# A convolution in 8 planes of 64 partitions: 64x64 products over 6 shifts instead of 128x128 products over 4

## The reference, cut to what matters

```python
qkv = conv2d(x, w_qkv)                       # 1x1, 256 -> 768 channels
agg = conv2d(qkv, w_dw, groups=768, pad=2)   # 5x5, each channel by itself
agg = conv2d(agg, w_pw, groups=96)           # 1x1 within groups of 8 channels
ms = concatenate([qkv, agg], axis=1)         # 64 heads of q, k, v with 8 channels each
q, k, v = split(...);  q = relu(q);  k = relu(k);  v = pad(v, one more column of ones)
kv = einsum('bgnd,bgne->bgde', k, v)
out = einsum('bgnd,bgde->bgne', q, kv)
out = out[..., :-1] / (out[..., -1:] + 1e-15)
return conv2d(out, w_proj)                   # 1x1, 512 -> 256
```

## Time and profile before

| | us |
|---|---|
| median of 3 runs | 9156.37 (9153.67 to 9159.21) |
| the profiled execution's own time | 9132.41 |
| its span, first to last instruction | 9130.6 |
| PE busy in the span | 7661.6 (84%) |
| DVE, POOL, ACT busy | 5047.8, 3797.0, 3522.8 |
| mean granted clock of PE | 0.910 |

### The profile page before, as it was taken

One profiled execution on the slowest core, in us unless ns is written; L12 is line 12 of the kernel. 1 busy time (PEld: TensorE's weight loads), 2 busy tenths in 40 slices (PEclk: granted clock), 3 DMA queues, 4 the chain that ended last, 5 costly groups with the idle time before them and its releaser, 6 DMA issues.

```text
span 9130.6 us, 206107 instructions
## 1 busy us (share of the span) xinstructions
PE 7661.6 (84%) x65004; PEld 5202.2 (57%) x65004; DVE 5047.8 (55%) x11563; ACT 3522.8 (39%) x9207; POOL 3797.0 (42%) x10084
## 2 busy tenths in 40 slices
PE   8978899788997879978899787997889978899778
PEld 5645566555565555555556555565555655555555
DVE  3475644756446564475644756447564465644656
ACT  1145621455214462144521455214452145521455
POOL 2335533355333553344533355334453344533444
PEclk9988899888998899988899889998899988999889
DMA  3201122011220112201122011220112201122111
GB/s 100 65 15 26 38 88 65 15 26 38 89 65 15 26 40 87 65 16 27 39 87 65 15 26 42 84 65 17 26 47 78 65 17 26 50 75 65 21 22 54
DMA packets 398743, 431.90 MB, mean 47 GB/s; under 512 B 159184, under 2 KB 355984, under 8 KB 393296
## 3 DMA queue, kind: packets, MB, share of 16 engines
q1 hardware_dynamic: 397648, 418.42, 16.2%
HBM read 102.76 MB, written 67.63 MB: 19 GB/s over the span
## 4 chain that ended last, share of the span: by engine, by line
PE 54%; DVE 23%; issue 7%; DMA 6%; ACT 5%; DVEq 3%; SPq 1%; POOL 1%; POOLq 0%; ACTq 0%
PE PS L621 12%; PE PS L684 7%; DVE arena L1132 5%; PE PS L902 5%; DVE arena L1222 4%; PE PS L771 4%; PE PS L867 3%; PE PS L664 3%; PE PS L827 3%; PE PS L836 3%; DVE SM L1346 3%; ACT arena L1076 2%; DVEq L1334 2%; PE PS L652 2%; DMA kv_rows<-arena 2%
## 5 line engine op out<-in xcount | busy, mean ns | idle before, releaser
L971 ACT ACTIVATE arena<-PS 128x128 f32<-128x128 f32 (+5 forms) x4160 | 1552.4, 399 | 2072.8 <-PE PS L621 598.2
L559 POOL COPY arena<-arena 64x129 f32 x6144 | 1537.7, 294 | 1386.7 <-PE PS L873 1136.1
L483 POOL TENSOR_TENSOR arena<-arena 128x512 f32<-128x512 f32 x768 | 806.4, 1072 | 1459.4 <-PE PS L621 1443.9
L621 PE MATMUL PS<-arena 128*128 128x256 f32 x6144 | 1360.3, 380 | 48.5 <-DMA arena<-arena 48.1
L1132 DVE COPY arena<-PS 64x260 f32<-64x260 f32 (+2 forms) x1272 | 634.4, 515 | 1362.4 <-PE PS L621 527.6
L621 PEld LDWEIGHTS PS<-arena 128*128 128x128 f32 x6144 | 1156.7, 189 | 272.9 <-issue 95.6
L1132 DVE COPY arena<-arena 64x129 f32 x4096 | 855.7, 271 | 414.5 <-PE PS L873 298.0
L807 PE MATMUL PS<-arena 64*64 64x192 f32 x8192 | 714.7, 391 | 249.5 <-POOL arena L559 227.6
L1222 DVE RECIPROCAL arena<-arena 128x512 f32<-128x512 f32 x256 | 857.6, 3350 | 119.0 <-ACT arena L1019 117.4
L489 POOL TENSOR_TENSOR BUF<-BUF,arena 128x512 f32<-128x512 f32 x256 | 358.5, 1400 | 1283.2 <-ACT arena L1007 1283.2
L1346 DVE TENSOR_REDUCE SM<-PS 128x1 f32<-128x384 f32 x1024 | 570.8, 557 | 540.2 <-issue 411.1
(11 more groups left out here) (102 smaller groups left out, 10581.1 us busy)
## 6 DMA issues: line engine op xcount, KB each, us to landing
arena<-arena SPq DMA_DIRECT2D x1024, 128.0 KB, 2.3
arena<-arena SPq DMA_DIRECT2D x768, 144.5 KB
BUF<-in_x SPq DMA_DIRECT2D x18, 2048.0 KB, 11.5
kv_rows<-arena SPq DMA_DIRECT2D x256, 130.0 KB, 3.5
arena<-kv_rows SPq DMA_DIRECT2D x256, 130.0 KB
out<-BUF SPq DMA_DIRECT2D x64, 512.0 KB, 2.6
arena<-in_taps SPq DMA_DIRECT2D x96, 288.0 KB, 3.7
W<-in_w SPq DMA_DIRECT2D x2, 768.0 KB, 5.6
```

Of the source, the lines that this page charges most:

```text
L483: last = pool.tensor_tensor(o, tap, mix, ALU.mult)
L559: last = pool.tensor_copy(G[p % GD][0:D, j // 3, j % 3, :], KVB[0:D, bass.ds(off, KVW)])
L621: last = nc.tensor.matmul(bank(i)[:, a * 256:(a + 1) * 256], lhsT=TW[n % 2][:, a * CH + k * P:a * CH + (k + 1) * P], rhs=src[:, k // 2:k / ...
L971: return nc.scalar.activation(o, i, ACT.Copy)
```

## The change

The image is split into 4x2 planes of 16x32 positions. A head is then 8 channels times 8 planes, 64 partitions, and two heads of a pair lie one above the other in one `IN` tile of 128 partitions. The stencil takes 2x3 = 6 shifts. A product has 64x64 weights; each pair has one for each of 6 shifts, 2 heads `a` and 2 halves `o` of the positions, 24 in all with 256 columns, and the four of a shift use the four quadrants of rows and columns of PE. A pair now fills two items, one per head, of half a bank each: ACT empties the one and DVE the other. The numbering of items follows. There are as many loads as before, of 64 partitions; stores are four per pair instead of two. GpSimd builds the weights in one product of 384 elements per partition. The taps and the views of planes follow the new split.

```diff
-PL, R = 16, 16
-PW = R + 1
-PAD = PW * PW
+PL, R, RC2 = 8, 16, 32
+PW, PC = R + 1, RC2 + 2
+PAD = PW * PC
+SHIFTS = 6
-I_QKV, I_SUM0, I_CQ, I_CKV, I_SUM1, I_LAST, HALF_ITEMS = 0, 24, 42, 50, 82, 98, 130
+I_QKV, I_SUM0, I_CQ, I_CKV, I_SUM1, I_LAST, HALF_ITEMS = 0, 24, 42, 58, 106, 122, 154
-TAPS = 72
+TAPS = 8 * SHIFTS + 8
 def conv_item(n):
-    return g * HALF_ITEMS + (I_CQ + m + 8 if m < 0 else I_CKV + m + 2 * max(0, (m - 2) // 2))
+    return g * HALF_ITEMS + (I_CQ + 2 * (m + 8) if m < 0 else I_CKV + 2 * m + 2 * max(0, (m - 2) // 2))
 def att_item(src, c):
-    return I_CKV + min(2 * c + 4, 16) + 2 * c if src == 0 else I_LAST + max(2 * c, 4 * c - 4)
+    return I_CKV + min(4 * c + 8, 32) + 2 * c if src == 0 else I_LAST + max(2 * c, 4 * c - 4)
...
-            return tile.rearrange("p (f r c) -> p f r c", f=PL, r=PW)[:, f:f + 2, oy:oy + R, ox:ox + R]
+            return tile.rearrange("p (f r c) -> p f r c", f=PL, r=PW)[:, c, oy:oy + R, 1:RC2 + 1]
-            return tile.rearrange("p (r fy c fx) -> p fy fx r c", fy=4, c=R, fx=4)[:, fy]
+            return tile.rearrange("p (r fy c fx) -> p fy fx r c", fy=4, c=RC2, fx=2)[:, fy]
...
 load_pair (SP):
                             wait_filled(sp, b, conv_item(n - 3))
+                            settle(sp)
+                            wait_filled(sp, b, conv_item(n - 3) + 1)
-                            sp.dma_start(IN[n % 3][:, a * PAD:(a + 1) * PAD],
+                            sp.dma_start(IN[n % 3][a * D:(a + 1) * D, :],
 store_pair (SP):
-                        sp.wait_ge(s_free[i % 2], b * IT + 2 + count(i, i % 2))
                         for a in range(2):
-                            sp.dma_start(head_rows(AGG[j], 2 * pr + a).rearrange("p (f n) -> p f n", f=PL),
-                                         OUTG[n % 3][:, a * 256:(a + 1) * 256]).then_inc(s_og[n % 3], 16)
+                            sp.wait_ge(s_free[a], b * IT + 2 + count(i + a, a))
+                            rows = head_rows(AGG[j], 2 * pr + a).rearrange("p (f n) -> p f n", f=PL)
+                            for o in range(2):
+                                sp.dma_start(rows[:, :, o * 256:(o + 1) * 256],
+                                             OUTG[n % 3][o * D:(o + 1) * D, a * 256:(a + 1) * 256]
+                                             ).then_inc(s_og[n % 3], 16)
 toeplitz (GpSimd):
                             wait_filled(pool, b, conv_item(n - 2))
+                            settle(pool)
+                            wait_filled(pool, b, conv_item(n - 2) + 1)
-                        for a in range(2):
...
-                            last = pool.tensor_tensor(o, tap, mix, ALU.mult)
-                        last.then_inc(s_tw, 1)
+                        tap = tap.unsqueeze(2).broadcast_to([P, SHIFTS, 8, 8])
+                        mix = dw[:, 8 * SHIFTS:].unsqueeze(1).unsqueeze(3).broadcast_to([P, SHIFTS, 8, 8])
+                        pool.tensor_tensor(o, tap, mix, ALU.mult).then_inc(s_tw, 1)
 conv (PE):
                                 claim(i)
+                                claim(i + 1)
-                                for a in range(2):
-                                    src = IN[n % 3][:, a * PAD:(a + 1) * PAD].rearrange("p (r c) -> p r c", r=PW)
-                                    for k in range(4):
+                                settle(pe)
+                                for k in range(SHIFTS):
+                                    for a, o in ((0, 0), (1, 1), (0, 1), (1, 0)):
+                                        head = slice(a * D, (a + 1) * D)
+                                        rows = IN[n % 3][head, :].rearrange("p (r c) -> p r c", r=PW)
+                                        y, xx = k // 3 + o * R // 2, k % 3
                                         last = nc.tensor.matmul(
-                                            bank(i)[:, a * 256:(a + 1) * 256],
-                                            lhsT=TW[n % 2][:, a * CH + k * P:a * CH + (k + 1) * P],
-                                            rhs=src[:, k // 2:k // 2 + R, k % 2:k % 2 + R],
-                                            start=(k == 0), stop=(k == 3))
-                                hand(i, last)
+                                            bank(i + a)[o * D:(o + 1) * D, 0:256],
+                                            lhsT=TW[n % 2][head, k * D:(k + 1) * D],
+                                            rhs=rows[:, y:y + R // 2, xx:xx + RC2],
+                                            start=(k == 0), stop=(k == SHIFTS - 1))
+                                        if k == SHIFTS - 1 and o != a:
+                                            hand(i + a, last)
 conv (ACT and DVE):
-                    i = conv_item(n)
-                    if i % 2 == e:
-                        wait_filled(eng, b, i)
-                        eng.wait_ge(s_og[n % 3], b * 512 + 32 * (n // 3 + 1))
-                        op(OUTG[n % 3], PS[:, i % 4, :]).then_inc(s_free[e], 1)
+                    i = conv_item(n) + e
+                    wait_filled(eng, b, i)
+                    eng.wait_ge(s_og[n % 3], b * 1024 + 64 * (n // 3 + 1))
+                    op(OUTG[n % 3][:, e * 256:(e + 1) * 256], PS[:, i % 4, 0:256]).then_inc(s_free[e], 1)
```

More of the change, by code:

```diff
@@ L162, in build @@
         AGG = [l0.take(L), l0.take(L), RAW[1][:, 0:L]]
-        IN = [l0.take(2 * PAD) for _ in range(3)]
+        IN = [l0.take(PAD) for _ in range(3)]
         OUTG = [l0.take(2 * 256) for _ in range(3)]
-        TW = [l0.take(2 * CH) for _ in range(2)]
-        DW = [l0.take(8 * TAPS) for _ in range(2)]
+        TW = [l0.take(SHIFTS * D) for _ in range(2)]
+        DW = [l0.take(4 * TAPS) for _ in range(2)]
         KTS = [l0.take(2 * P) for _ in range(2)]
@@ L204, in chunk_of @@
         def chunk_of(tile, c):
-            f = 2 * c
-            oy, ox = f // 8, (f % 4) // 2
-            return tile.rearrange("p (f r c) -> p f r c", f=PL, r=PW)[:, f:f + 2, oy:oy + R, ox:ox + R]
+            oy = c // 4
+            return tile.rearrange("p (f r c) -> p f r c", f=PL, r=PW)[:, c, oy:oy + R, 1:RC2 + 1]
         def head_rows(tile, a):
@@ L224, in planes @@
         def planes(ap):
-            return ap.rearrange("p (f r c) -> p f r c", f=2, r=R)
+            return ap.rearrange("p (r c) -> p r c", r=R)
         def natural(tile, fy):
-            return tile.rearrange("p (r fy c fx) -> p fy fx r c", fy=4, c=R, fx=4)[:, fy]
+            return tile.rearrange("p (r fy c fx) -> p fy fx r c", fy=4, c=RC2, fx=2)[:, fy]
         def x_planes(X, kt, c):
-            f = 2 * c
-            return natural(X[:, kt, :], f // 4)[:, f % 4:f % 4 + 2]
+            return natural(X[:, kt, :], c // 2)[:, c % 2]
         s_w = sem("weights_loaded")
@@ L335, in _ @@
             for s in s_og:
-                sp.sem_inc(s, 32)
+                sp.sem_inc(s, 64)
             for kt in range(KT):
@@ L451, in clear_halo @@
             def clear_halo(j):
-                tile = RAW[j].rearrange("p (oy y ox x r c) -> p oy y ox x r c", oy=2, y=2, ox=2, x=2, r=PW)
-                by_oy = RAW[j].rearrange("p (oy f r c) -> p oy f r c", oy=2, f=8, r=PW)
+                by_oy = RAW[j].rearrange("p (oy f r c) -> p oy f r c", oy=2, f=4, r=PW)
                 for oy in range(2):
                     pool.memset(by_oy[:, oy, :, R - R * oy, :], 0.0)
-                    for ox in range(2):
-                        last = pool.memset(tile[:, oy, :, ox, :, oy:oy + R, R - R * ox], 0.0)
+                    for side in (0, PC - 1):
+                        last = pool.memset(by_oy[:, oy, :, oy:oy + R, side], 0.0)
                 last.then_inc(s_zero, 1)
@@ L672, in wait_stored @@
                             for k in range(3):
-                                pe.wait_ge(s_og[k], b * 512 + 32 * ((n - k) // 3 + 2))
+                                pe.wait_ge(s_og[k], b * 1024 + 64 * ((n - k) // 3 + 2))
                         for j in range(3):
@@ L961, in norm_chunk @@
             if layer == 0:
-                return (XN[:, kt, :].rearrange("p (fy fx r c) -> p fy fx r c", fy=4, fx=4, r=R)[:, q],
+                return (XN[:, kt, :].rearrange("p (fy fx r c) -> p fy fx r c", fy=4, fx=2, r=R)[:, q],
                         natural(X[:, kt, :], q))
@@ L1440 @@
     plane = (np.arange(4) + 2) % 4
-    t = 4 * np.arange(2)[None, :, None] + plane[:, None, None] - np.arange(4)[None, None, :] + 3
-    tt = padded[:, t[:, :, :, None, None, None], t[None, None, None]]
-    tt = tt.transpose(0, 1, 4, 2, 5, 3, 6).reshape(96, 8 * 16, 64)
+    ty = 4 * np.arange(2)[None, :, None] + plane[:, None, None] - np.arange(4)[None, None, :] + 3
+    tx = 2 * np.arange(3)[None, :, None] + np.arange(2)[:, None, None] - np.arange(2)[None, None, :] + 3
+    tt = padded[:, ty[:, :, :, None, None, None], tx[None, None, None]]
+    tt = tt.transpose(0, 1, 4, 2, 5, 3, 6).reshape(96, D, 8 * SHIFTS)
     pw = np.asarray(inputs["L0_conv_w_pw"])[perm, :, 0, 0].reshape(96, 8, 8)
```

(6 more changed lines are left out.)

9 lines of the change are left out of this document (3 added, 6 removed).

## The result

| | before | after |
|---|---|---|
| median, first comparison (4 runs each) | 9155.02 | 9208.88 (9189.23 to 9216.61) |
| the profiled execution's own time, span | 9132.41, 9130.6 | 9189.23, 9187.4 |
| ratio after / before, 95% interval | | 1.0057 [1.0037, 1.0077] |
| ratio when measured once more on another occasion | | 1.0095 [1.0078, 1.0112] |

The forecast was 9085 us, in a range from 8965 to 9205. The change makes the kernel slower: by 54 us in the first comparison, 34 to 70 by the interval. PE's work fell as forecast, and it doesn't show in the time.

The account below looks back on a forecast made before the run. PE was taken to bound the convolution, with SP's queue and banks binding after the change. First parts -10, second parts 0, planes -56, start -5: -71, so 9061 profiled and 9085 us for the timed median; range 8965 to 9205.

Parts of the forecast that it names:

- Four quadrants at a time, 2.6 us a pair: Convolution on PE: matmuls on four different quadrants run side by side, a pair takes 2.6 us, 0.9 less than before.
- SP's queue in part 1, "44.9 us against 45.5": Pairs 0 to 11 of each convolution: SP's DMA issues set the pace, 44.9 us against 45.5; -10 us in all.
- The price c: SP's time for one 64-row DMA issue in the convolution: taken as 0.60 us, between 0.46 and 0.65.
- Half the rows: Convolution DMAs: 64 rows instead of 128 argued for an issue price of 0.60 us, below the old 0.65.
- The bank chain in part 2, "8.6 us after the last": Pairs 12 to 23: PE waits for DVE to release the attention chunk's banks; cycle 8.6 us against 8.63, no gain.
- The planes, -56: Second group's last stage: DVE reads x at step 2 at the contiguous price, about 7 us a batch, 56 saved.
- The start of a batch, -5: Start of each batch: normalisation's first quarter shortens and PE waits less, 0.6 us x 8 = 5 saved.
- B: Convolution: SP's queue becomes the bound everywhere, deciding from 0.65 us an issue; 9160 us, 9266 at 0.70; chance 0.22.
- A: Convolution: SP's issues get really cheap, up to 0.52 us; pairs 0 to 11 take 37.4 to 40.6, total 8965 to 9017; chance 0.26.
- C: DVE's views of x: a step of 2 costs like a step of 4, so no gain there; 9146 us; chance 0.10.
- D: Convolution: PE's clock or quadrants fail, each pair takes 5.2 us, +590 us; chance 0.06.
- one of the signs of being wrong: Convolution stage: PE's clock at half level within it was listed as showing the forecast wrong; no size given.

Follow-up runs that it names:

- ACT's stores alone: Changed kernel with the two stores of each pair's first head issued by ACT instead of SP; 9076 us, ratio 0.9937 to the kernel before.
- six banks alone: Changed kernel, all issues on SP, with the first layer's PSUM items rotating over six banks instead of four; ratio 1.0042 to the kernel before.
- plain transfers with ACT's stores: Changed kernel with ACT issuing the first head's stores and pair transfers plain, 64 whole rows both sides (wrong rows moved); ratio 0.9880 to the kernel before.

## Why the prediction was wrong, step by step

- *Four quadrants at a time, 2.6 us a pair*: right, 8.00 us for three pairs.
- *SP's queue in part 1, "44.9 us against 45.5"*: this step failed. It named the right bound and took each of its terms a little short. By the rows, part 1 is 3.35 us to the first store (102.24; 3.1 taken), 39.99 for the issues up to the end of pair 11's loads at 142.23 (37.5 taken with the taps), 2.82 from there to PE's start at 145.05 (1.7 taken) and 2.76 for pair 11 (2.6): 48.92. The price c itself was near: 0.61 for a store and 0.66 for a load where 0.60 was taken, 0.708 per issue with its gap instead of 0.68. The two taps loads, each also shifting the queue, and a short stall cost 1.8 us instead of 0.8, and the landing 1.1 more. The mean of 49.6 is 0.7 above this stage; the three first parts with the lowest clock (0.90) took 49.5 to 52.3 us, the six at 0.97 48.8 to 49.6, so PE's clock has a part in it. In all +4.3 us a stage where -0.6 was forecast, 4.9 x 16 = 78 us of the miss. "Half the rows" had no weight at all: an issue of this structure costs the same with 128 rows, with 64 and with half the bytes.
- *The bank chain in part 2, "8.6 us after the last"*: the mechanism was right and its size was off. From the chunk's first matmul to the reciprocal 1.79 us (1.69 taken), then 3.47, and from the division's start to the pair's start 1.04 (0.79 taken), the pair 2.75 (2.6), so 9.05. Over six cycles it is 55.74 us against 51.85; two of the six cycles are longer still (9.23 and 10.18 us), and there PE starts 2.8 to 3.0 us behind SP's loads, which came late: behind four stores that took 3.82 us instead of 2.67, and behind a taps load and slower issues. The forecast was no change, and it was +3.6 us a stage, 57 us of the miss. A tie between old and new cycle (8.63 and 8.6) should have been priced as a risk on one side only: the old cycle had nothing to lose, the new one three unpriced hand-overs.
- *The planes, -56*: right, -6.5 us a batch, -52.
- *The start of a batch, -5*: nothing came of it. PE's waits for DVE's first quarter shrink from 35.2 to 31.4 us over the eight batches, but the stretch from its first projection to the first group's convolution is 0.5 us a batch longer (61.6 against 61.1). Why wasn't looked into.
- *The rivals*: B, slower by SP's queue, is what happened in part 1, at a lower c than the 0.65 from which it was said to decide. In part 2 it wasn't SP first but the bank chain, with SP right behind: that B's cycle of 9.0 us fits the 9.05 measured is luck. Of A, the floor of 3.3 to 3.5 us a pair by eight engines exists and shows once the stores are on ACT, as 41.1 us at full clock for the 12 pairs (3.4 each) where about 38 was reckoned. C is out. Of D a small part is true, and with it one of the signs of being wrong: the clock was at half level for about one pair in part 1, up to about three in others, which an idle time of 2.11 us before the change didn't bring.

Everything that PE gave back (240 us of busy time) thus went into waiting for two chains: SP's issues, which the old pace of 3.5 us a pair had hidden with 0.55 us to spare, and the banks, which only the new numbering of items brought onto PE's path.

## What to carry to other kernels

When a change makes the bound engine's step shorter, work out the next two bounds of that step, each with its hand-overs, and count DMA issues per step before anything else: one queue gave one issue per 0.64 to 0.71 us here, with 64 KB as with 32, and halving a transfer to fit a layout doubles that. Two bounds that lie close must be lifted together: against the changed kernel ACT's stores alone gave 1.2 to 1.6%, six banks alone 0.1 to 0.5%, both 3.0 to 3.4%. Look too at how many partitions the narrower side of a small transfer has: with 4 the packets ran four at a time here, with 8 eight, with 64 up to sixteen.

## What the runs showed of the hardware that was not expected

- The price of an issue goes with the structure of its access, not with rows or bytes: minimum of a store 461 to 464 ns plain (64 and 128 rows), 546 with 4 x 16 rows on one side, 608 with 8 x 16 or 8 x 8. The medians of plain ones in a busy queue are 531 to 596.
- A store with 4 partitions on one side instead of 8, cheaper to issue, lengthened part 1 by 5.9 us (55.2 against 49.3).
- With waits of 1.4 to 2.4 us between pairs of 64x64 matmuls the granted clock was 0.90 to 0.97 over part 1; at its lower level a pair took 4.51 us (its records from 114.10) instead of 2.8. With the same PE work and shorter or fewer waits (plain transfers with ACT's stores) it was 1.00 in 9 of the 16 first parts.
- Packets on twice as many engines took longer each: 160 ns against 94 for 2312 bytes, at 160 against 146 GB/s.
